# A two-layer graph network on one core: SyncE carries a chunk every twelve units, and the convolution finishes one tile of nodes a turn

## The reference, cut to what matters

```python
h = maximum(layernorm(x), 0)
# layer 0: for each type t
xw = (h + emb_table[node_type]) @ W[t]
e  = leaky_relu((xw @ att_src[t])[src] + (xw @ att_dst[t])[dst])
# softmax of e over the edges of type t (and a self edge) of each destination
out_sum += segment_sum(w_edge * xw[src]) / denom + bias[t]
x = x + out_sum
# layer 1
h = maximum(layernorm(x), 0)
filters  = silu(edge_attr @ fW1 + fb1) @ fW2 + fb2
messages = (h[src] @ dW + db) * filters
aggregated = segment_sum(messages, dst)
x = x + h + silu(aggregated @ uW1 + ub1) @ uW2 + ub2
```

## Time and profile before

| | |
|---|---|
| runs | 5,419.4, 5,423.0, 5,437.2 us; median 5,423.0 |
| profiled execution, span | 4,155.8 us (no other time is given for it) |
| median less span | 1,267.2 us |
| GpSimd busy | 3,070.8 us, 74% |
| TensorE busy, mean granted clock | 3,395.1 us, 82%, 0.60 |
| VectorE, ScalarE busy | 57%, 33% |
| gathers of GpSimd | 1,604 in each edge stage |

### The profile page before, as it was taken

One profiled execution on the slowest core, in us unless ns is written; L12 is line 12 of the kernel. 1 busy time (PEld: TensorE's weight loads), 2 busy tenths in 40 slices (PEclk: granted clock), 3 DMA queues, 4 the chain that ended last, 5 costly groups with the idle time before them and its releaser, 6 DMA issues.

```text
span 4155.8 us, 58597 instructions
## 1 busy us (share of the span) xinstructions
PE 3395.1 (82%) x13945; PEld 2624.2 (63%) x13946; DVE 2388.6 (57%) x5253; ACT 1364.7 (33%) x3361; POOL 3070.8 (74%) x3239
## 2 busy tenths in 40 slices
PE   5788788888888888888777888888888888788888
PEld 3566666666666666666555666666666666667666
DVE  7888888888888888888842322322332323223223
ACT  5455555555555555555411111111111111111111
POOL 5777777777777777777657777777777777777775
PEclk7555555555555555555577666676666666766667
DMA  4222222222222222222223222222222222222222
GB/s 124 56 59 61 59 59 61 60 59 61 59 59 61 59 59 61 59 59 61 58 60 98 77 74 76 71 76 75 71 76 73 74 75 72 75 76 71 76 74 79
DMA packets 180619, 286.01 MB, mean 69 GB/s; under 512 B 82273, under 2 KB 123054, under 8 KB 176011
## 3 DMA queue, kind: packets, MB, share of 16 engines
q0 software_dynamic: 102656, 213.73, 19.6%
q1 hardware_dynamic: 77856, 71.32, 6.1%
HBM read 271.06 MB, written 12.49 MB: 68 GB/s over the span
## 4 chain that ended last, share of the span: by engine, by line
POOL 36%; issue 12%; POOLq 1%; PE 1%; DMA 0%; DVE 0%; DVEq 0%
POOL ce_xg L63 36%; POOLq L676 0%; PE ce_ring L1429 0%; PE ce_ps_h L1420 0%; PE ce_ring L1420 0%; POOLq L677 0%; PE ce_ps_h L1407 0%; POOLq L688 0%; PE ce_ring L1385 0%; DMA ce_xg<-table,ce_idx 0%; POOLq L1275 0%; DVE ce_msg L1466 0%; POOLq L686 0%; DVE sums L1519 0%; DVEq L1275 0%
## 5 line engine op out<-in xcount | busy, mean ns | idle before, releaser
L63 POOL DMA_INDIRECT ce_xg<-table,ce_idx x1604 | 1520.8, 948 | 498.4 <-issue 488.9
L63 POOL DMA_INDIRECT ae_xg<-table,ae_idx x1604 | 1517.5, 946 | 501.8 <-issue 501.5
L1466 DVE TENSOR_TENSOR ce_msg<-ce_ring,ce_xg 128x768 f32<-128x768 f32 x269 | 257.7, 958 | 1333.7 <-DMA ce_xg<-table,ce_idx 1333.3
L924 PE MATMUL ae_ps_k<-ae_xg,ae_e 128*96 128x129 f32 x3224 | 882.4, 432 | 0.0
L1397 PE MATMUL ce_ps_h<-ce_ea,ce_fw 50*128 50x384 f32 x1076 | 611.9, 706 | 258.3 <-DMA ce_ea<-in_edge_attr 257.3
L1339 ACT ACTIVATE ce_hid<-ce_ps_h,ce_fb 128x768 f32<-128x768 f32 x269 | 242.5, 901 | 1749.6 <-PE ce_ps_h L1397 1749.6
L924 PEld LDWEIGHTS ae_ps_k<-ae_xg,ae_e 128*96 128x96 f32 x3224 | 689.4, 277 | 126.5 <-issue 117.1
L1376 PEld LDWEIGHTS ce_ring<-ce_fw,ce_hid 128*128 128x128 f32 x3228 | 582.2, 276 | 290.4 <-issue 151.8
L1376 PE MATMUL ce_ring<-ce_fw,ce_hid 128*128 128x128 f32 x3228 | 650.9, 376 | 65.5 <-DVE ce_msg L1466 65.4
L1385 PEld LDWEIGHTS ce_ring<-ce_hot,ce_msg 128*128 128x128 f32 x3224 | 521.1, 250 | 4.4 <-DVE ce_msg L1466 4.2
L1385 PE MATMUL ce_ring<-ce_hot,ce_msg 128*128 128x32 f32 x3224 | 507.3, 316 | 2.5 <-DVE sums L1474 2.5
(11 more groups left out here) (181 smaller groups left out, 3235.8 us busy)
## 6 DMA issues: line engine op xcount, KB each, us to landing
ce_ea<-in_edge_attr SPq DMA_DIRECT2D x90, 450.0 KB
ae_xg<-table,ae_idx POOLq DMA_INDIRECT x1604, 2.5
ce_xg<-table,ce_idx POOLq DMA_INDIRECT x1604, 2.5
ae_stage<-table SPq DMA_DIRECT2D x1024, 0.5 KB
ce_stage<-table SPq DMA_DIRECT2D x1024, 0.5 KB
sums<-in_x SPq DMA_DIRECT2D x7, 448.0 KB, 5.1
table<-sums SPq DMA_DIRECT2D x6, 462.0 KB, 3.6
pj_bias<-in_x_rows SPq DMA_DIRECT2D x42, 64.0 KB
```

Source lines behind the costliest of these rows:

```text
L63: eng.indirect_dma_start(out=out, out_offset=None, in_=table[:, :], in_offset=bass.IndirectOffsetOnAxis(ap=idx, axis=0)).then_inc(done, 16)
L924: last = nc.tensor.matmul(ps_k[0:KEYS, 0:D + 1], by_chunk[s % 3][:, c, :], xg[:, s % XS, c, 0:D + 1], start=(c == 0), stop=(c == count - 1))
L1466: nc.vector.tensor_tensor(msg[:, s % 3, :, :], filt, xg[:, s % XS, :, :], ALU.mult).then_inc(s_msg, 1)
```

## The change

Four things are changed.

- SPAN is 2 and CARRIED is 20: the carried chunk comes every second turn, twelve units, twenty times a stage instead of eight.
- The lists of all carried chunks are read once, and scaled once to byte offsets (by GpSimd in `prepare`, by VectorE ahead of the convolution). `collect` loads sixteen values at a time and issues each row by bytes, without an operation on registers. It runs in four shares of 32 rows.
- In SyncE's half turn the stores of attention's tile (now `behind`) and the wait for the carried chunk's landing stand after the share of rows.
- The convolution's loop finishes one tile a turn from turn 2 on: TensorE's two products (L1419 of the new kernel among the hidden filters, L1396 among the filters of slot 3), one activation, two additions of VectorE and one store. After the loop the last group of seven remains, in two halves. The six loads of finished tiles all stand in turn 1.

```diff
-SPAN = 5
-SPANS = TURNS // SPAN
-CARRIED = SPANS - 1
+SPAN = 2
+CARRIED = 20
 CARRY_SLOT = 4
+READ = 16
...
-    def collect(self, nc, sp, table, b, q):
-
-        todo = range(q * P // (SPAN * LOADS), (q + 1) * P // (SPAN * LOADS))
-        for first in range(todo[0], todo[-1] + 1, 8):
-            part = range(first, min(first + 8, todo[-1] + 1))
-            rows = nc.values_load_multi_w_load_instructions(
-                self.lists[:, b, part[0]:part[-1] + 1], engines=[mybir.EngineType.SP], min_val=0, max_val=N - 1,
+    def collect(self, nc, sp, t, b, q):
+
+        share = P // (SPAN * LOADS)
+        size = 4 * self.width
+        for first in range(q * share, (q + 1) * share, READ):
+            starts = nc.values_load_multi_w_load_instructions(
+                self.lists[:, bass.ds(t * P + first, READ)], engines=[mybir.EngineType.SP], min_val=0, max_val=(N - 1) * size,
                 skip_runtime_bounds_check_because="a source is a node")[1]
-            for p, row in zip(part, rows):
-                sp.dma_start(self.stage[p:p + 1, b, :], table[bass.ds(row, 1), :]).then_inc(self.rows_in, 16)
+            for p, start in enumerate(starts, first):
+                sp.dma_start(self.stage[p:p + 1, b, :].bitcast(u8), self.bytes[:, bass.ds(start, size)]).then_inc(self.rows_in, 16)
...
-            if q == 0:
-                if not first:
-                    deliver(r, t, b)
-                sp.wait_ge(carry.list_in, 16 * (r * CARRIED + t + 1))
-                carry.read_list(sp, a, t + 2, b)
-                if not first:
-                    sp.wait_ge(carry.carried, 16 * (r * CARRIED + t))
-                    sp.sem_inc(carry.turn, 1)
-            carry.collect(nc, sp, table, 1 - b, q)
+            if q == 0 and not first:
+                deliver(r, t, b)
+            if q == 0 and first:
+                listed()
+            carry.collect(nc, sp, t, 1 - b, q)
+            if v == 0:
+                behind(r, SPAN * t + j)
+            if q == 0 and not first:
+                sp.wait_ge(carry.carried, 16 * (r * CARRIED + t))
+                sp.sem_inc(carry.turn, 1)
...
+            pool.wait_ge(lists_in, 16)
+            nc.gpsimd.tensor_scalar(row_starts(state), row_starts(state), 4.0 * ROW, None, ALU.mult)
...
+                        if opens(i) and s == 1:
+                            k = r * DONE + i - OPEN
+                            act.wait_ge(t_u, k + 1)
+                            if not (isinstance(i, int) and i == OPEN):
+                                act.wait_ge(t_v, k)
+                            nc.scalar.activation(one_hid[:, :], tile_u, ACT.Silu, bias=update.b1[:, :]).then_inc(t_hid, 1)
...
+                        if opens(i) and s == 1:
+                            pe.wait_ge(s_acc, r * UNITS + i * SL - 4)
+                            nc.tensor.matmul(tile_u, update.w1[:, :], acc[:, bass.ds((i - OPEN) * P, P)], start=True, stop=True).then_inc(t_u, 1)
...
+                    if s == UPDATE_SLOT and opens(i):
+                        update_tile(i)
...
+                def update_tile(i):
+
+                    k = r * DONE + i - OPEN
+                    if isinstance(i, int) and i == OPEN:
+                        dve.wait_ge(y_in, 16 * (GROUPS - 1) * (r + 1))
+                    else:
+                        dve.wait_ge(out_done, 16 * k)
+                    nc.vector.tensor_tensor(done[:, :].unsqueeze(1), by_tile[:, bass.ds(i - OPEN, 1), :], update.b2[:, :].unsqueeze(1), ALU.add).then_inc(t_bias, 1)
+                    dve.wait_ge(t_v, k + 1)
+                    dve.wait_ge(t_bias, k + 1)
+                    nc.vector.tensor_tensor(done[:, :], done[:, :], tile_y, ALU.add).then_inc(t_y, 1)
...
+            def beside(r, i):
+
+                if closes(i):
+                    sp.wait_ge(t_y, r * DONE + i - OPEN)
+                    sp.dma_start(out[bass.ds((i - OPEN - 1) * P, P), :], done[:, :]).then_inc(out_done, 16)
```

More of the change, by code:

```diff
@@ L549, in landed_by, with carry_turns @@
     return r * 16 * gathers + 16 * (SPAN * CH - 1) * carried + 16 * CH * j + 16 * CH
-def carry_turns(eng, body, apart=0):
+def carry_turns(eng, body):
     body(0, True, SL, 0)
[L555 to L559, removed]
+    for i in range(1, 2 * SPAN):
+        body(i, False, SL, i // SPAN)
+    with eng.Fori(2, CARRIED) as t, eng.Fori(0, SPAN) as j:
         body(SPAN * t + j, False, SL, t, j)
@@ L582, in __init__ @@
         self.lists = lists
-        self.rows_in, self.list_in, self.carried = sem("rows_in"), sem("list_in"), sem("carried")
+        self.bytes = table.rearrange("n r -> (n r)").rearrange("(o x) -> o x", o=1).bitcast(u8)
+        self.rows_in, self.carried = sem("rows_in"), sem("carried")
         self.turn = project.carry_turn
@@ L648, in load_indices @@
         span(r, 0, 0, True)
-        with sp.Fori(0, CARRIED // 2 - 1) as p:
+        span(r, 1, 1)
+        with sp.Fori(1, CARRIED // 2) as p:
+            span(r, 2 * p, 0)
             span(r, 2 * p + 1, 1)
-            span(r, 2 * p + 2, 0)
-        span(r, CARRIED - 1, 1)
-        for q in range((SPAN - 1) * LOADS):
+        for q in range((TURNS - 1 - SPAN * CARRIED) * LOADS):
             j, v = divmod(q, LOADS)
             following(r, SPAN * CARRIED + j, v)
+            if v == 0:
+                behind(r, SPAN * CARRIED + j)
             if q == 0:
                 deliver(r, CARRIED, 0)
+        sp.wait_ge(carry.carried, 16 * (r + 1) * CARRIED)
+        sp.sem_inc(carry.turn, 1)
         for v in range(LOADS):
@@ L683, in gather_units @@
         turn(0, True, SL)
-        with pool.Fori(1, SPAN) as i:
+        for i in range(1, SPAN):
             turn(i, False, SL)
-        with pool.Fori(1, SPANS - 1) as t:
+        with pool.Fori(1, CARRIED) as t:
             turn(SPAN * t, False, SL, t)
-            with pool.Fori(1, SPAN) as j:
+            for j in range(1, SPAN):
                 turn(SPAN * t + j, False, SL)
@@ L772, in beside, with behind @@
                     sp.dma_start(p.x[:, :], a["x_rows"][bass.ds((i - OPEN) * P, P), :]).then_inc(x_in, 16)
+            def behind(r, i):
                 if closes(i):
@@ L779, in _ @@
             sp.sem_inc(stored, 32)
-            load_indices(nc, sp, a, h, idx, idx_in, gathered, landed, carry, table, xg, s_sum, beside=beside)
+            load_indices(nc, sp, a, h, idx, idx_in, gathered, landed, carry, xg, s_sum, beside=beside, behind=behind)
             passes = pass_count(sp, h)
@@ L1338, in turn @@
                             act.wait_ge(s_flt, n - 2)
+                        if opens(i) and s == 1:
[4 more added lines that the diff above has]
+                            nc.scalar.activation(one_hid[:, :], tile_u, ACT.Silu, bias=update.b1[:, :]).then_inc(t_hid, 1)
                         nc.scalar.activation(hid[:, b, :].rearrange("p (k e) -> p k e", k=2), ps_h[:, :].rearrange("p (k e) -> p k e", k=2)[:, :, 0:H],
                                              ACT.Silu, bias=fb1[:, :]).then_inc(s_act, 1)
-                turns(act, turn)
-            def hidden(g, s, fresh):
-                act.wait_ge(s_u, g + 1)
-                if not fresh:
-                    act.wait_ge(s_v, g - 1)
-                nc.scalar.activation(up_hid[:, s, :].rearrange("p (k n) -> p k n", k=2), ps_u[s][:, :].rearrange("p (k n) -> p k n", k=2)[:, :, 0:half],
-                                     ACT.Silu, bias=update.b1[:, :]).then_inc(s_up_hid, 1)
-            act.wait_ge(update.loaded, 64)
-            hidden(0, 0, True)
-            hidden(1, 1, True)
-            with act.Fori(0, (GROUPS - 3) // 2) as i:
-                hidden(2 * i + 2, 0, False)
-                hidden(2 * i + 3, 1, False)
-            hidden(GROUPS - 1, 0, False)
+                finishing_turns(act, turn)
+            for k, (a0, a1) in enumerate(HALVES):
+                act.wait_ge(s_u, k + 1)
+                nc.scalar.activation(up_hid[:, a0 * P:a1 * P], ps_u[:, a0 * P:a1 * P], ACT.Silu, bias=update.b1[:, :]).then_inc(s_up_hid, 1)
         @block.gpsimd
@@ L1374, in filters @@
                         pe.wait_ge(key_ready, r + 1)
+                    if i is not None and opens(i) and s == UPDATE_SLOT:
+                        pe.wait_ge(t_hid, r * DONE + i - OPEN + 1)
+                        nc.tensor.matmul(tile_y, one_hid[:, :], update.w2[:, :], start=True, stop=True).then_inc(t_v, 1)
                     for c in range(CH):
@@ L1399, in turn @@
                         if not (first and s < 1):
-                            filters(n - 1, (s - 1) % SL, first and s < 3)
+                            filters(n - 1, (s - 1) % SL, first and s < 3, i if s else None)
                         if not (first and s < 3):
                             sums(n - 3, (s - 3) % SL, first and s < 5)
-                turns(pe, turn)
+                finishing_turns(pe, turn)
                 n = (r + 1) * UNITS
```

124 lines of the change are left out of this document (52 added, 72 removed).

## The result

| | before | changed |
|---|---|---|
| median | 5,424.0 us (4 runs, 5,419.4 to 5,437.2) | 5,577.5 us (4 runs, 5,572.4 to 5,593.4) |
| ratio | | 1.029, 95% interval 1.027 to 1.031: slower |
| profiled execution, its time | not given | 5,572.4 us |
| its span | 4,155.8 us | 5,570.5 us |
| GpSimd busy | 3,070.8 us, 74% | 3,055.6 us, 55% |

The change lost 153 us where 48 were to be gained. One row of the table already says which number of the prediction can't stand: the changed kernel's span and time differ by 1.9 us, not by 1,267. The rows ahead of the prediction came from an execution of 4,156 us, in other conditions than the runs that they were set against.

The account below looks back on a forecast made before the run. The prediction took GpSimd's unbroken gathers, about 1.25 us each, to bound the kernel; 15.0 + 15.0 us for fewer gathers and 18.0 for the tail, 48.0 in all, took 5423.0 to 5375.0 us, range 5350 to 5403.

Parts of the forecast that it names:

- I work with the span and take the remainder as fixed: Whole kernel: the 1,267.2 us between span and median lie around the span and stay.
- The first rival: Both stages: the 1,267 us scale with the gathers, giving 5363 us; chance 0.25.
- SyncE still waits for GpSimd and its cost on the path is nothing: SyncE's half turns: 15.1 us in attention, 15.9 in the convolution, plus 0.6 for stores, below GpSimd's 22.2; cost nothing.
- the cover is gone at 0.54: SyncE's half turn: with 32 rows it fills GpSimd's 22.2 us once a row costs 0.54 us.
- the prediction's formula: SyncE's half turn: 4.2 us in attention or 5.0 in the convolution, plus 32 rows at their price.
- the second rival: Both stages: SyncE becomes the pace; at 0.60 us a row 208 us slower, 5631; chance 0.08.
- its signs: SyncE as the pace would show as GpSimd waiting for an index load, rows above 0.5 us apart.
- Gathers taken away: GpSimd, both stages: 12 gathers fewer in each, saving 15.0 us and 15.0 us.
- Tail: After the convolution's loop: only the last group of seven remains, saving 18.0 us; bounds 15 and 18.2.
- The update in the loop at no cost: Convolution's loop: one tile a turn costs nothing; a late store may hold VectorE a few us, with 37 us slack.
- The scaling of the lists in the prologue: GpSimd in the prologue: scaling 2,560 list values takes 7.2 us, hidden; bound 0 to 3 us.
- The rule weighed: Convolution: VectorE's 42 two-input bias additions hold up no gather, price zero; the rival's 12 us, 5387, had chance 0.03.

Follow-up runs that it names:

- conditions A: Not one run: the conditions in which the kernel before takes 4,152 to 4,158 us.
- conditions B: Not one run: the conditions in which the kernel before takes 5,419 to 5,486 us.
- s4b: Repeat of the changed kernel with ten carried chunks a stage, 16 rows a half turn: 5,376.5 us, ratio 0.9888 to the kernel before.
- a1: The changed kernel again, unaltered, beside the kernel before at 5,433.4 us: 5,576.2 us.
- f_carry: The changed kernel's carrying alone (20 chunks a stage), update behind the loop as in the kernel before: 5,690.1 us, one run.
- f_update: The kernel before with only the update moved into the convolution's loop, eight chunks carried: 5,502.4 us, one run.
- a0: The changed kernel again, unaltered, beside the kernel before at 4,155.7 us: 4,106.4 us, ratio 0.9884.
- s4: The changed kernel with SPAN 4 and CARRIED 10, so 16 rows a half turn: 5,433.7 us, beside 5,485.0 for the kernel before.
- e_update: The kernel before with only the update moved into the convolution's loop, eight chunks carried: 4,135.4 us, ratio 0.9956.

## Why the prediction was wrong

**The steps that failed** are two. The first is "I work with the span and take the remainder as fixed, since nothing in the change touches what lies outside". There was no outside. Time and span differ by 2 us in every execution that has both (4,156.9 and 4,155.1 in A, 5,572.4 and 5,570.5 in B), so the trace that all terms were read from was one of conditions A and the median that they were subtracted from one of conditions B. The first rival, gathers slower in proportion, was as wrong: a gather takes 947 ns in both, and what lies between two of them is a wait that A doesn't have.

**SyncE** is the second, and the one that made the loss: "SyncE still waits for GpSimd and its cost on the path is nothing". The prediction took 0.34 us a row, bounds 0.27 and 0.41, from rows of A, and wrote that the cover is gone at 0.54. In A a row takes 0.33, 0.37 with its list load, and the price was right. Its reading of the cover was not quite: it divided SyncE's waits by all 88 halves. With the eight that carry nothing taken out (157.9 and 156.5 us of the kernel before), the halves with rows had 12.3 and 11.5 us left, not 13.0 and 12.2. After the change they have 6.7 and 6.1, where it foresaw 7.1 and 6.3. In B the same rows take 24.3 and 26.8 us a half. By the prediction's formula the halves then are 4.2 + 24.3 = 28.5 us in attention and 5.0 + 26.8 = 31.8 in the convolution (somewhat too much, as its 4.2 and 5.0 hold the list loads already). With SyncE out of the way a half takes 29.1 and 28.7 in B (17.75 x 1.641 and x 1.615, from s4b's starts, 61.7 to 2688.9 and 2753.1 to 5339.1 with 1,602 gathers each). Attention just fits; the convolution doesn't. The measured half there is 17.75 x 1.744 = 31.0 us, 2.3 over, times 80 halves is 183 us; a1 and s4b lie 200 apart. So the second rival was the mechanism, with its price and its formula, in the stage where SyncE has the attribute loads as well, and its signs came: rows over 0.5 us apart, GpSimd waiting for index loads. It had 0.08, because "every one of 2,048 rows took 224 to 322 ns to issue"; that was true of one condition.

**Gathers taken away.** In A the last starts came 17.8 and 33.7 us sooner (2048.7 against 2066.5, 4089.2 against 4122.9); 15.0 and 30.0 were foretold. Of the 3.7 us more, 3 are a slightly closer row in attention (1.249 us). In B attention took, from the first start to the last, 2,678 us with 1,592 gathers (f_carry) beside 2,701 with 1,604 (f_update), but 2,636 with 1,592 (a1) beside 2,627 with 1,602 (s4b). One trace each: no steady gain from a gather less shows there.

**Tail.** In A the last group's first addition starts at 4098.20, 3.1 us after the first product; before, it was 21.2: 18.1 saved, 18.0 foretold. From the last gather to the end it is 13.2 us against 32.9, 19.7 saved.

**The update in the loop at no cost** held in A: VectorE's wait for the store of the tile before came as described and was longer than "a few us" (307.5 / 41 = 7.5 us), and went out of its wait for gathered rows (946.3 us where the earlier trace rows had 1,333.3): the stage took no more. The scaling of the lists in the prologue took 6.68 us for 7.2.

**The rule weighed.** In a0 the convolution's gathers stand 1.254 us apart beside 42 new bias additions of VectorE, 1.253 before. The Trainium skill ("SBUF — State Buffer", section "Who interferes with whom") would have each of them hold up a gather, if a gather counts as a GpSimd instruction that reads SBUF: 42 x 0.29 = 12 us, or 1.261 us apart. The trace of the change doesn't show it either. The same section also says that VectorE's two-input operation was not seen to stall the making of GpSimd's descriptors, which the prediction left out and which agrees with these rows.

Sum of the parts in A: 33.7 + 19.7 = 53.4 us of span, 49.3 between the medians, for 48.0. (a0's trace is of the fastest of its four runs.) The sum was right for a run that it wasn't made against.

## What to carry to other kernels

When the profiled span and the median don't agree, find out first whether they are of the same conditions: a remainder of a quarter of the time is a finding, not a constant. Cover worked out from one trace is cover in that trace; an engine whose half turn was filled to seven tenths with small instructions became the pace when its instructions got dearer. A smaller share (ten chunks, not twenty) won in conditions B, where the full share lost; in A it would keep about half of the gain by the sum of the parts (23 of 49 us). Ask of every cover what is queued behind it: here 32 rows that no one was in a hurry for stood ahead of an index load that everyone waited for.

## What the runs showed of the hardware

- One and the same kernel takes 4,152 to 4,158 or 5,419 to 5,486 us, with nothing between. It isn't a matter of the chip alone: a0 and s4 ran on chips of the same number, the kernel before at 4,156 and at 5,485.
- In the slower conditions the data work of VectorE, ScalarE and GpSimd is as fast as ever: a gather 947 ns, silu of 768 columns 900 ns, VectorE's multiplication 957 ns. So are the signals that VectorE gives: 34 ns to ScalarE and 57 to TensorE, 33 and 55 in A. Late are TensorE's results (4.2 us instead of 0.17 from product to silu, 4.1 with nothing carried) and SyncE's instructions (a register move with its step 337 ns instead of 60).
- It is no matter of what SyncE moves: an empty loop's round of three instructions took 0.86 us. How long that loop takes in A wasn't measured.
- The mean granted clock of TensorE was 0.55 to 0.57 there and 0.59 to 0.61 in A. No run shows whether that is a cause or follows from TensorE's waits.
- Open: what makes TensorE's results and SyncE's instructions late. Every execution whose span is known was recorded by the profiler, so the recording itself may have a part in it. Records are lost in B: of 26 signals that are each raised 269 times, the trace of e_update has 270 records in the median and that of f_update 193, and 102 of the waits before silu have no releaser ("remote") in f_update, none in e_update. The Trainium skill ("NOTIFIC — the notification-queue block", section "Overflow: three behaviours, one of which stalls the engine") says that the block through which such records leave may, when a queue is full, hold back the engine that makes them. Steps that come late whatever the instruction does would fit it. Against it, the section gives dropping and holding back as alternatives, and here VectorE and ScalarE lose records without being late. No run here was made without recording, so none shows it.
- Open too: why eight carried chunks cost 72 us in B (5,485.0 against 5,412.6), below the threshold, where ten of the cheaper rows cost 27 (5,433.7 against 5,406.9, the update in the loop in both), one run each.
